# Two LSTM recurrences and the attention behind them: which sum stands in front of the state, and where three steps of a slot stand

## The reference

```
xW = einsum('bsd,gd->sbg', x, Wih) + b
def step(carry, xt):
    h, c = carry
    i, f, g, o = split(xt + h @ Whh.T)
    c = sigmoid(f) * c + sigmoid(i) * tanh(g)
    h = sigmoid(o) * tanh(c)
q = mlp(lstm(x, ..._q)); k = mlp(lstm(x, ..._k))      # relu between two linear layers
out = softmax(causal(q @ k.T / 8)) @ v                # 16 heads of 64, 4 key heads
x = x + out @ Wo.T
```

## Time and profile before

| | |
|---|---|
| time, three runs | 2543.56, 2552.73, 2553.86 us; median 2552.73 |
| profiled execution | 2545.53 us, span 2544.2 us |
| recurrences' first and last product | 70.3 and 450.8 us |
| attention stage L0Attn | 453.2 to 606.3 us |
| busy share of the span | PE 80%, DVE 56%, ACT 33%, POOL 15% |
| L1301, products of the recurrences | 10,752 in 306.3 us |

### The profile page before, as it was taken

How to read it: one execution, slowest core, us unless ns; L and a number is a source line. 1 busy time by engine, 2 the same in 40 slices (tenths; PEclk the granted TensorE clock), 3 DMA queues, 4 the chain that set the end, 5 groups by cost and what they waited for, 6 DMA issues and landing times.

```text
span 2544.2 us, 56331 instructions
## 1 busy us (share of the span) xinstructions
PE 2037.6 (80%) x22708; PEld 1478.9 (58%) x22708; DVE 1426.9 (56%) x3903; ACT 840.5 (33%) x2961; POOL 388.3 (15%) x655
## 2 busy tenths in 40 slices
PE   7877877887878799388794688799889999879734
PEld 3777777776556566245683565466554545656522
DVE  5677777564425588633461561577427130578787
ACT  1333333342216466010241452366311011246411
POOL 2111111121001100000231550233000000310011
PEclk9555555798888899699997898899999999789956
DMA  3000000103000000200003000000030000000000
GB/s 124 4 4 4 4 4 4 70 1 157 9 0 2 10 11 8 124 1 0 5 1 133 1 2 1 10 11 7 1 140 1 0 0 1 1 14 14 1 0 15
DMA packets 7744, 57.13 MB, mean 22 GB/s; under 512 B 760, under 2 KB 5216, under 8 KB 5728
## 3 DMA queue, kind: packets, MB, share of 16 engines
q1 hardware_dynamic: 7488, 53.54, 5.4%
HBM read 52.62 MB, written 0.92 MB: 21 GB/s over the span
## 4 chain that ended last, share of the span: by engine, by line
PE 61%; issue 16%; DVE 13%; ACT 4%; POOL 4%; DMA 2%; POOLq 0%; DVEq 0%; SPq 0%; ACTq 0%
PE banks L251 33%; PE banks L1301 12%; PE banks L256 7%; PE banks L890 2%; PE banks L916 2%; ACT memory L1476 2%; DVE memory L1200 1%; PE banks L1448 1%; DVE memory L777 1%; DMA memory<-in_l2x_rows 1%; ACT memory L938 1%; DVE memory L976 1%; DVE memory L2629 1%; DVE memory L1403 1%; DVE memory L1492 1%
## 5 line engine op out<-in xcount | busy, mean ns | idle before, releaser
L251 PE MATMUL banks<-memory 128*112 128x256 f32 (+7 forms) x4192 | 1143.1, 428 | 105.2 <-ACT memory L1610 13.5
L251 PEld LDWEIGHTS banks<-memory 128*128 128x128 f32 (+3 forms) x4192 | 710.5, 197 | 446.2 <-issue 256.4
L256 PE MATMUL banks<-memory 112*125 112x112 f32 (+3 forms) x2000 | 311.3, 289 | 192.9 <-DVE memory L777 107.1
L256 PEld LDWEIGHTS banks<-memory 112*125 112x125 f32 (+3 forms) x2000 | 241.1, 174 | 308.0 <-issue 180.9
L1301 PE MATMUL banks<-memory 128*128 128x8 bf16 (+2 forms) x10752 | 306.3, 174 | 75.8 <-DVE memory L1403 74.4
L1301 PEld LDWEIGHTS banks<-memory 128*128 128x128 bf16 x10752 | 295.3, 104 | 87.4 <-DVE memory L1403 85.3
L938 ACT ACTIVATE memory<-banks,memory 112x375 f32<-112x375 f32 x384 | 215.1, 578 | 25.3 <-DVE memory L976 25.1
L976 DVE TENSOR_REDUCE memory<-banks 112x2 f32<-112x750 f32 x192 | 171.0, 933 | 47.6 <-PE banks L890 45.9
L984 DVE COPY memory<-banks 125x448 f32<-125x448 f32 x192 | 116.5, 618 | 10.5 <-PE banks L256 6.1
L1325 ACT ACTIVATE memory<-memory 128x64 f32<-128x64 f32 x224 | 57.4, 256 | 171.7 <-DVE memory L1386 171.7
L1350 POOL TENSOR_SCALAR memory<-memory 128x16 f32<-128x16 f32 x224 | 59.8, 267 | 343.3 <-DVE memory L1403 343.3
(11 more groups left out here) (221 smaller groups left out, 2275.5 us busy)
## 6 DMA issues: line engine op xcount, KB each, us to landing
memory<-in_l2x SPq DMA_DIRECT2D x1, 7680.0 KB, 21.5
memory<-in_l2f SPq DMA_DIRECT2D x1, 7168.0 KB, 19.4
memory<-in_l1f SPq DMA_DIRECT2D x1, 4617.0 KB, 14.3
memory<-in_ctxT SPq DMA_DIRECT2D x24, 187.5 KB
memory<-in_l0a SPq DMA_DIRECT2D x1, 4224.0 KB, 15.9
memory<-in_l2f SPq DMA_DIRECT2D x1, 4096.0 KB, 13.1
memory<-in_l3f SPq DMA_DIRECT2D x1, 3073.0 KB, 22.3
memory<-in_l2a SPq DMA_DIRECT2D x1, 3072.0 KB, 18.4
```

Source lines behind the costliest of these rows:

```text
L251: ins = self.nc.tensor.matmul(out, weights[i], acts[i], start=i == 0, stop=i == n - 1)
L256: return self.nc.tensor.transpose(out, in_, self.ident[0:n, 0:n])
```

## The change

In the recurrences: the gates' order becomes f, i, g, o, so that o is last; the sum over the slots becomes two, one of six blocks (192 to 48 columns) and one of o's two blocks (64 to 16), each with PSUM slots in banks of its own. PE signals after block 5 of the last pass and again at its end. ACT takes tanh in two instructions and copies the input in two; each state waits for both tanhs. On DVE o's sum of recurrence 1 stands behind recurrence 0's second part. The third part of the state moves from DVE to POOL, ahead of the keep. The weights are scaled in three instructions instead of two.

In the attention: `y` moves from the front of `EVEN` to its end. `hid` moves into `ODD`, behind `v`, for the batch element of the next slot; a slot -1 is added for the first one.

```diff
--- before.py
+++ after.py
@@ -1262,7 +1263,8 @@
         self.upper = [self.h[:, l].rearrange("p s c -> p (s c)").bitcast(BF16).rearrange(
             "p (s c two) -> p s c two", s=3, two=2)[:, :, :, 1] for l in range(2)]
         flat = k.banks.rearrange("p n c -> p (n c)")
-        self.slots = [flat[:, 1024 * l + 320:1024 * l + 576].rearrange("p (s c) -> p s c", s=4) for l in range(2)]
+        at = lambda first, n: flat[:, first - 3 * n * B:first + n * B].rearrange("p (s c) -> p s c", s=4)
+        self.slots = [(at(1024 * l + 512, 6), at(1024 * l + 2560, 2)) for l in range(2)]
 
     def run(self):
         self.dve()
@@ -1298,19 +1300,24 @@
                         PE.wait_ge(*s.h_parts(2 * t + l - 1))
                     for g in range(GT):
                         for j in range(KD):
+                            own, first = (self.slots[l][0], 0) if g < 6 else (self.slots[l][1], 6)
+                            at = (g - first) * B
                             ins = self.nc.tensor.matmul(
-                                self.slots[l][:, part:3, g * B:(g + 1) * B], whh[:, part, l, j, g * P:(g + 1) * P],
-                                self.upper[l][:, 0:3 - part, j * B:(j + 1) * B], start=part == 2 and g == 0 and j == 0,
+                                own[:, part:3, at:at + B], whh[:, part, l, j, g * P:(g + 1) * P],
+                                self.upper[l][:, 0:3 - part, j * B:(j + 1) * B], start=part == 2 and g == first and j == 0,
                                 stop=j == KD - 1 and part == 0, skip_group_check=True)
+                        if part == 0 and g == 5:
+                            ins.then_inc(*s.gates_full.up())
                 ins.then_inc(*s.gates_full.up())
 
     def act(self):
         k, s, A = self.k, self.s, self.nc.scalar
         A.wait_ge(*k.landed["l0a_whh"].now())
         for l in range(2):
-            A.activation(self.raw[:, l, :, 0:6 * P], self.raw[:, l, :, 0:6 * P], ACT.Copy, scale=0.25)
-            A.activation(self.raw[:, l, :, 6 * P:8 * P], self.raw[:, l, :, 6 * P:8 * P], ACT.Copy,
-                         scale=0.5).then_inc(*s.whh_scaled.up())
+            for at, n, scale in ((0, 4, 0.25), (4, 2, 0.5), (6, 2, 0.25)):
+                blocks = self.raw[:, l, :, at * P:(at + n) * P]
+                ins = A.activation(blocks, blocks, ACT.Copy, scale=scale)
+            ins.then_inc(*s.whh_scaled.up())
         for l in range(2):
             A.wait_ge(*s.whh_scaled(l + 1))
             A.copy(self.whh[:, 0, l], self.raw[:, l]).then_inc(*s.whh_a.up())
@@ -1318,20 +1325,27 @@
             A.copy(self.whh[:, 1, l], self.raw[:, l]).then_inc(*s.whh_a.up())
         A.wait_ge(*s.gates_sum(4 * self.GT))
         for l in range(2):
-            self.act_input(0, l)
+            self.act_input(0, l, 0)
+            self.act_input(0, l, 1)
         for t in range(S):
             for l in range(2):
-                A.wait_ge(*s.gates_in(2 * t + l + 1))
-                A.activation(self.gates[:, l, 1:5, :].rearrange("p g c -> p (g c)"), self.sums[:, l],
+                n = 2 * t + l
+                A.wait_ge(*s.gates_in(2 * n + 1))
+                A.activation(self.gates[:, l, 1:4, :].rearrange("p g c -> p (g c)"), self.sums[:, l, 0:6 * B],
                              ACT.Tanh).then_inc(*s.act_tanh.up())
+                A.wait_ge(*s.gates_in(2 * n + 2))
+                A.activation(self.gates[:, l, 4, :], self.sums[:, l, 6 * B:8 * B], ACT.Tanh).then_inc(*s.act_tanh.up())
                 if t + 1 < S:
-                    self.act_input(t + 1, l)
+                    self.act_input(t + 1, l, 0)
                 A.wait_ge(*s.cell_ready(2 * t + l + 1))
                 A.activation(self.tc[:, l], self.gates[:, l, 0], ACT.Tanh, scale=0.5).then_inc(*s.tc_ready.up())
-
-    def act_input(self, t, l):
-
-        self.nc.scalar.copy(self.slots[l][:, 3, :], self.xW[:, l, t, :]).then_inc(*self.s.xw_in.up())
+                if t + 1 < S:
+                    self.act_input(t + 1, l, 1)
+
+    def act_input(self, t, l, last):
+
+        src = self.xW[:, l, t, 6 * B:8 * B] if last else self.xW[:, l, t, 0:6 * B]
+        self.nc.scalar.copy(self.slots[l][last][:, 3, :], src).then_inc(*self.s.xw_in.up())
 
     def pool(self):
         k, s, G = self.k, self.s, self.nc.gpsimd
@@ -1346,6 +1360,9 @@
             G.tensor_tensor(self.whh[:, 2, l], self.raw[:, l], self.whh[:, 1, l], ALU.subtract).then_inc(*s.whh_g.up())
         for t in range(S):
             for l in range(2):
+                h, upper = self.h[:, l], self.upper[l]
+                G.wait_ge(*s.h_mid(2 * t + l + 1))
+                G.tensor_tensor(h[:, 2], h[:, 1], upper[:, 1], ALU.subtract).then_inc(*s.h_parts.up())
                 G.wait_ge(*s.h_hi(2 * t + l + 2))
                 G.tensor_scalar(self.hs[:, l, :, :, t], self.h[:, l, 0].rearrange("p (k b) -> p k b", k=KD), 0.5, None,
                                 ALU.mult).then_inc(*s.h_kept.up())
@@ -1362,34 +1379,35 @@
                 V.wait_ge(*s.up_full(at + 1))
                 dst = self.xW[:, l].rearrange("p t (g b) -> p g b t", g=GT)[:, g, half * HALF:(half + 1) * HALF, :]
                 V.tensor_scalar(dst, k.bank(at % 4, P, HT).rearrange("p (b t) -> p b t", b=HALF),
-                                self.bias["b_lstm"][:, n:n + 1], 0.5 if g < 6 else 1.0, ALU.add,
+                                self.bias["b_lstm"][:, n:n + 1], 1.0 if g in (4, 5) else 0.5, ALU.add,
                                 ALU.mult).then_inc(*s.gates_sum.up())
         V.memset(self.gates, 0.0)
         V.memset(self.h, 0.0).then_inc(*s.h_hi.up())
         V.wait_ge(*s.h_hi(1))
         for t in range(S):
-            self.dve_gates(t, 0)
+            self.dve_gates(t, 0, 0, 6)
+            self.dve_gates(t, 0, 6, 8)
             self.dve_cells(t, 0)
-            self.dve_gates(t, 1)
+            self.dve_gates(t, 1, 0, 6)
             self.dve_state(t, 0)
             self.dve_middle(t, 0)
+            self.dve_gates(t, 1, 6, 8)
             self.dve_cells(t, 1)
-            self.dve_low(t, 0)
             self.dve_state(t, 1)
             self.dve_middle(t, 1)
-            self.dve_low(t, 1)
-
-    def dve_gates(self, t, l):
+
+    def dve_gates(self, t, l, first, end):
         s, V = self.s, self.nc.vector
-        V.wait_ge(*s.xw_in(2 * t + l + 1))
-        V.wait_ge(*s.gates_full(2 * t + l + 1))
-        V.tensor_reduce(self.sums[:, l], self.slots[l].rearrange("p s c -> p c s"), AX,
+        last = first > 0
+        V.wait_ge(*s.xw_in(2 * (2 * t + l) + 1 + last if t else 2 * l + 1 + last))
+        V.wait_ge(*s.gates_full(2 * (2 * t + l) + 1 + last))
+        V.tensor_reduce(self.sums[:, l, first * B:end * B], self.slots[l][last].rearrange("p s c -> p c s"), AX,
                         ALU.add).then_inc(*s.gates_in.up())
 
     def dve_cells(self, t, l):
         s, V, gates, prod = self.s, self.nc.vector, self.gates[:, l], self.prod[:, l]
-        V.wait_ge(*s.act_tanh(2 * t + l + 1))
-        V.scalar_tensor_tensor(out=prod, in0=gates[:, 1:3, :], scalar=1.0, in1=gates[:, 0:5:4, :], op0=ALU.add,
+        V.wait_ge(*s.act_tanh(2 * (2 * t + l) + 1))
+        V.scalar_tensor_tensor(out=prod, in0=gates[:, 1:3, :], scalar=1.0, in1=gates[:, 0:4:3, :], op0=ALU.add,
                                op1=ALU.mult).then_inc(*s.vstep.up())
         V.wait_ge(*s.vstep.now())
         V.scalar_tensor_tensor(out=gates[:, 0], in0=prod[:, 0], scalar=0.5, in1=prod[:, 1], op0=ALU.mult,
@@ -1397,21 +1415,17 @@
 
     def dve_state(self, t, l):
         s, V = self.s, self.nc.vector
+        V.wait_ge(*s.act_tanh(2 * (2 * t + l) + 2))
         V.wait_ge(*s.tc_ready(2 * t + l + 1))
         if t:
             V.wait_ge(*s.h_kept(2 * t + l - 1))
-        V.scalar_tensor_tensor(out=self.h[:, l, 0], in0=self.gates[:, l, 3], scalar=1.0, in1=self.tc[:, l], op0=ALU.add,
+        V.scalar_tensor_tensor(out=self.h[:, l, 0], in0=self.gates[:, l, 4], scalar=1.0, in1=self.tc[:, l], op0=ALU.add,
                                op1=ALU.mult).then_inc(*s.h_hi.up())
 
     def dve_middle(self, t, l):
         s, V, h, upper = self.s, self.nc.vector, self.h[:, l], self.upper[l]
         V.wait_ge(*s.h_hi(2 * t + l + 2))
         V.tensor_tensor(h[:, 1], h[:, 0], upper[:, 0], ALU.subtract).then_inc(*s.h_mid.up())
-
-    def dve_low(self, t, l):
-        s, V, h, upper = self.s, self.nc.vector, self.h[:, l], self.upper[l]
-        V.wait_ge(*s.h_mid(2 * t + l + 1))
-        V.tensor_tensor(h[:, 2], h[:, 1], upper[:, 1], ALU.subtract).then_inc(*s.h_parts.up())
 
 
 class Causal(Attention):
@@ -1533,10 +1547,10 @@
 class L0Attn(Causal):
 
     units = 2
-    EVEN = (("y", 0, 3), ("turn", 0, 2), ("sc", 0, 1), ("max", 0, 1), ("exp", 0, 1), ("hid", 0, 0), ("hid", 1, 0),
-            ("values", 0, 2), ("queries", 0, 0), ("inv", 0, 1))
+    EVEN = (("turn", 0, 2), ("sc", 0, 1), ("max", 0, 1), ("exp", 0, 1), ("queries", 0, 0), ("values", 0, 2),
+            ("inv", 0, 1), ("y", 0, 3))
```

(6 more changed lines are left out.)

## The result

The changed kernel takes 2517.86 us (median, 2511.6 to 2518.62); the kernel before, on the same chip, 2551.31. The ratio is 0.9869, 95% interval 0.9841 to 0.9896: 33 us less. Forecast were 2511 us and a range of 2499 to 2527. The profiled execution took 2511.6 us (span 2510.3), 33.9 less than that of before.

A forecast was written before the change was run, and what follows sets the result against it. Bounds: the recurrences' hand-over loop (PE, sum, state, PE) and two PE stalls per attention slot pair. Profiled 2545.5 us less 19 and 18 gave 2508.5, plus 3 for the median 2511; range 2499 to 2527.

The forecast's parts named there:

- Hand-over: Recurrences: earlier signal (0.11 us) and shorter sum (0.066) save 0.175 us in each of 111 hand-overs, 19.4 us.
- What has to stay hidden: Recurrences: both states and the third part stay ready in time, slack 0.2, 0.2 and 0.3 us.
- rival 2: Recurrences: GpSimd's third part holds up VectorE's cell of recurrence 1, gain only 8 us, 2522 us; chance 0.12.
- The extra waits: Recurrences: the state's wait for o's tanh passes during the sum, cost 0, at worst 0.03 us, 3 us in all.
- Attention: Layer 0's self attention: both PE stalls go, a slot pair takes 14.08 us instead of 16.73; 18.3 us less.
- The pair without new rows: Attention's last pair before the drain: 12.7 us in place of 16.7, gain 4.0 us.
- the drain: Attention's end: one turn and values move ahead of `y` into PE's idle time, gain 2 to 5 us, taken as 3.
- the start: Attention's beginning: more work stands ahead of the first `y`, some of it regained at the end, -2 us.
- Rival 1: Attention: odd round or bank ring stalls PE once a pair, 1 to 1.5 us; gain 10, 2519 us; chance 0.13.
- rival 4: Recurrences: the busier PE lifts its clock to full, 21 us more gain, 2490 us; chance 0.05.
- The sum: Whole kernel: -19 and -18 make -37 from 2545.5 profiled, 2508.5; plus 3 for the median, 2511 us.
- rival 3: Recurrences: GpSimd's subtraction costs 0.94 to 1.02 us, steps take 3.6 us, +6 in all, 2558 us; chance 0.04.

The follow-up runs named there:

- late_sig: Changed kernel, but PE signals only once, at the end of the 48 products, and both sums wait for that: 2526.35 us, ratio 0.9902.
- fewer_waits: Changed kernel without VectorE's wait for the input copy ahead of the first sum, from t = 1 on: 2506.97 us, ratio 0.9848.
- rec_only: Changed kernel with the attention's old order, so only the recurrences' change is left: 2539.09 us, ratio 0.9943.
- hid_only: Kernel before with only the hidden rows moved a slot ahead; `y` stays at the slot's front: 2561.27 us, ratio 1.0033.
- y_only: Kernel before with only `y` moved to the end of the even half; the hidden rows stay: 2542.91 us, ratio 0.9963.

## Why the prediction was right, step by step

- **Hand-over** (0.175 us a step, 19.4 us): right in mechanism and size, a step is 3.23. Of it 0.11 is the early signal (`late_sig`). Over the stage it is 17.0 us: 1.2 went into five slow steps, which I had not seen, and in the profiled execution the input products in front took 1.2 longer (PE's first product at 71.52, before at 70.27).
- **What has to stay hidden**: recurrence 1's state 1.15 behind (forecast 1.12), third part with 0.34 us of slack (0.3), no growth of VectorE's row beside GpSimd, so rival 2 is out. One reading was off: I put GpSimd's work at 0.56 of 3.2 us, but there are two recurrences in a step; it was busy 105.11 of 366 us, 0.93 a step, and nothing waited for it. The sentence of the Trainium skill (GPSIMD Engine Reference, Key points) on contention is not borne out with two inputs on both sides: L1410 takes 0.18 us beside the subtraction, and 0.19 alone.
- **The extra waits** I priced at 0 to 0.03. The state's cost nothing on the path (the state stands 0.28 behind the sum, 0.34 before, with a sum 0.066 shorter). That the second wait in front of a sum has a price of 0.06 I had not seen; it was there in the kernel before too, and `fewer_waits` showed it.
- **Attention** (18.3): 20.4. A pair takes 13.90 and not 14.08. From the first `y` to the sixth it is 15.7 us for my 13.3: 2.8 to 3.1 four times, and 4.2 in the fifth, which has no hidden rows of a next slot in it any more. The pair without new rows gave 3.4 (4.0), the drain 3.5 (3), the start -2.2 (-2). That PE would set the pace is shown by 69.45 of 70 us busy. Rival 1 is out.
- **Clock** (rival 4): PEclk in the recurrences stayed at 0.51 with PE 84% busy. The Trainium skill's rule (TensorE: Matmul & The Clock Gate, HAM clock gate) that activity releases the throttle did not show itself here.
- **The sum**: -37 forecast, -33.9 between profiles, -33.4 between medians. That the two stages gave 37.4, as the sum said, is partly luck: the recurrences gave 2 us less than forecast and the attention 2 more. Other stages then took 3.5 back, which no term had. The point of 2511 was 7 too low, half for this and half for its anchor: I added 3 us to the profiled execution, whose median lay 7 above it. 2552.73 - 37 = 2515.7 would have been nearer.
- **Two numbers of the prediction** that moved nothing: the stages that the diff does not touch are 2544.2 - 380.5 - 153.1 = 2011 us and not 1990, and rival 3 stands at 2558 by the median of before, where by the sum's own anchor its +6 gives 2555.

## What to carry to other kernels

Where two chains share an engine queue, look at what stands between an operation and the moment its input was there, and shorten *that*; an engine's total work may grow (VectorE's sums by 149 ns each time) and the time still fall. A step whose result nobody in the round needs must not stand in the round. Moves that each remove idle time need not add up while PE's clock can fall: try them apart and together, and compare stages, since a gain of 0.6% of the whole (`rec_only`, 14 us) is near what untouched stages vary by.

## What the runs showed of the hardware

- VectorE paused at multiples of 128 of its own instructions, up to 0.37 us in the trace, on the path or not according to where the pause fell. With 16 instructions a step, which divides 128 (kernel before and `fewer_waits`), no step was slow; that the pause then always fell in one and the same covered place is argued and not seen.
- Where an operation on the path had two waits, one of them became an instruction of its own, and the operation started 0.06 us later, though the other wait had long been fulfilled.
- In one order (`hid_only`) a single pause of PE of 1.64 us in a pair was followed by half clock each time; in the kernel before two pauses of 0.86 and 1.79 were not. The order does not decide alone: in `rec_only`, whose attention is that of the kernel before, half clock for 3.4 us came with one of the six pauses of 1.8 (`y` then took 5.08 us), and in `y_only` behind one of the four of 1.17. What decides it stays open.
- Stages with the same code took between 65.5 and 73.1 us (layer 3's self attention), and between 273.7 and 279.2 (the two of layer 2), with 20 to 43 and 14 to 31 us at half clock. Such differences are as large as the 10 us between executions of one kernel; why an execution gets one or the other was not tried.
